# Layer 4 of a conditioned residual stack: expert slots sorted by expert and taken in couples of 256 columns

## The reference

```
x += layer1: expert e = argmax(cond_8[b]):  (silu(x Wup_e + b) * (x Wgate_e + b)) Wdown_e + b    (hidden 256)
x += layer2: x W_base + b + 2 * sum_e cond_8[b,e] * (x A_e) B_e                                  (rank 16)
x += layer3: x (sum_g cond_8[b,g] * weight_g * mask) + bias
x += layer4: sum over the 2 best experts of b: w * (gelu(x Gate_e) * (x Up_e)) Down_e            (hidden 512)
             + the same gated unit with shared weights, for all batches
```

## Time and profile before

| | |
|---|---|
| median of 3 runs | 167.18 us (166.98 to 167.9) |
| the profiled execution, its span | 166.84 us, 165.0 us |
| TensorE busy | 160.8 us (97%) |
| VectorE, ScalarE, GpSimd busy | 84.0 us (51%), 50.0 us (30%), 16.2 us (10%) |
| granted TensorE clock | 1.000 of full |
| DMA | 35.31 MB, mean 214 GB/s |

### The profile page before, as it was taken

How to read it: one execution, slowest core, us unless ns; L and a number is a source line. 1 busy time by engine, 2 the same in 40 slices (tenths; PEclk the granted TensorE clock), 3 DMA queues, 4 the chain that set the end, 5 groups by cost and what they waited for, 6 DMA issues and landing times.

```text
span 165.0 us, 3603 instructions
## 1 busy us (share of the span) xinstructions
PE 160.8 (97%) x1202; PEld 147.9 (90%) x1202; DVE 84.0 (51%) x171; ACT 50.0 (30%) x97; POOL 16.2 (10%) x20
## 2 busy tenths in 40 slices
PE   6999999999999999999999999999999999999994
PEld 2369989999999999999999999999999999999993
DVE  2903665667995362564634364643634563543632
ACT  3656434460542222122222222122222222122120
POOL 2099790000000000000000000000000000000000
PEclk9999999999999999999999999999999999999999
DMA  3999889999801847458684847587494849100001
GB/s 95 405 370 377 318 282 333 312 420 421 368 11 25 344 143 256 183 200 223 223 273 152 308 139 273 182 259 214 174 283 136 319 116 311 44 0 4 0 0 64
DMA packets 8962, 35.31 MB, mean 214 GB/s; under 512 B 1144, under 2 KB 2424, under 8 KB 8824
## 3 DMA queue, kind: packets, MB, share of 16 engines
q1 hardware_dynamic: 8528, 33.99, 59.0%
q10 hardware_dynamic: 424, 1.20, 1.8%
HBM read 34.14 MB, written 1.05 MB: 213 GB/s over the span
## 4 chain that ended last, share of the span: by engine, by line
PE 97%; DVE 1%; issue 0%; POOL 0%; DVEq 0%; POOLq 0%
PE pair L400 35%; PE acc L421 17%; PE pair L393 13%; PE pair L342 9%; PE acc L415 7%; PE acc L351 4%; PE pair L315 3%; PE pair L331 2%; PE pair L372 2%; PE pair L379 2%; PE acc L300 2%; DVE hid L516 0%; PE acc L307 0%; POOL zeros L227 0%; PE acc L326 0%
## 5 line engine op out<-in xcount | busy, mean ns | idle before, releaser
L400 PE MATMUL pair<-x,ring 128*128 (+1 forms) x512 | 62.2, 275 | 0.0
L400 PEld LDWEIGHTS pair<-x,ring 128*128 128x128 f32 x512 | 59.7, 192 | 0.1
L290 ACT ACTIVATE act<-pair 128x512 f32<-128x512 f32 x48 | 28.6, 597 | 85.6 <-PE pair L400 60.3
L563 DVE SCALAR_TENSOR_TENSOR hid<-pair,w_col,act 128x512 f32<-128x512 f32 x32 | 23.9, 751 | 40.2 <-PE pair L400 40.2
L421 PE MATMUL acc<-hid,ring 128*128 128x128 f32 x256 | 33.6, 275 | 0.0
L421 PEld LDWEIGHTS acc<-hid,ring 128*128 128x128 f32 x256 | 32.3, 192 | 1.4
L567 DVE TENSOR_TENSOR hid<-pair,act 128x512 f32<-128x512 f32 x16 | 11.1, 692 | 16.9 <-PE pair L393 16.9
L342 PE MATMUL pair<-x,ring 128*128 x128 | 16.7, 276 | 0.3 <-issue 0.3
L342 PEld LDWEIGHTS pair<-x,ring 128*128 128x128 f32 x128 | 15.5, 192 | 0.5 <-issue 0.5
L516 DVE SCALAR_TENSOR_TENSOR hid<-pair,ring,act 128x128 f32<-128x128 f32 x32 | 9.8, 347 | 9.9 <-PE pair L342 9.7
L279 ACT ACTIVATE act<-pair,ring 128x128 f32<-128x128 f32 x32 | 10.0, 364 | 11.2 <-PE pair L342 11.2
(11 more groups left out here) (62 smaller groups left out, 106.9 us busy)
## 6 DMA issues: line engine op xcount, KB each, us to landing
ring<-experts SPq DMA_DIRECT2D x32, 768.0 KB, 4.4
ring<-experts SPq DMA_DIRECT2D x16, 386.5 KB, 4.6
x<-xT ACTq DMA_DIRECT2D x1, 1024.0 KB, 6.1
shared_sb<-shared SPq DMA_DIRECT2D x1, 768.0 KB, 6.7
out<-x SPq DMA_DIRECT2D x4, 192.0 KB, 4.3
w_sb<-w SPq DMA_DIRECT2D x1, 512.0 KB, 4.0
out<-x SPq DMA_DIRECT2D x4, 64.0 KB, 4.3
small_sb<-small ACTq DMA_DIRECT2D x1, 137.0 KB, 3.9
```

Source lines behind the costliest of these rows:

```text
L290: act.activation(act3[:, u % PAIRS, :], pair[u % PAIRS][0][:, :], ACT.Gelu_apprx_tanh)\
L400: ins = pe.matmul(bank[:, m * P:(m + 1) * P], ring3[:, slot, base + m * P:base + (m + 1) * P], x[:, cols(g * GB + c)], start=True, stop=True)
L563: dve.scalar_tensor_tensor(hid3[:, s, :], pair[s][1][:, :], w_col[:, bass.ds(g * GB + (k[0] * B + c), 1)], act3[:, s, :], ALU.mult, ALU.mu ...
```

## The change

The 32 pairs of batch and expert (slots) are sorted by expert. Each expert's slots are coupled two by two, and what can't be is left single; 12 couples and 8 singles always hold all 32. A couple's two batches are gathered side by side, so that its expert is multiplied with 256 columns in split float32r, in three matmuls for each block of weights. A couple has two units D (two of the four blocks of hidden features each); singles stay R units in float32. Shared units S are as before.

What changes by engine:

- VectorE computes the sort in a chain of small operations after the routing weights, and reads 32 batch numbers into registers ahead of `linear`. In layer 4 it takes the product and the low part of each split unit, and adds each couple's and single's result, times its weight, to `x_sum`, a copy of x.
- TensorE has two matmuls for the ranks, two for the sorted rows, and reads 8 batch numbers.
- SP reads 24 + 8 + 24 numbers, loads 12 + 8 expert packs, gathers 2 x 12 pieces of 128 KB from `x_hl` to `x_duo`, and stores all results at the end.
- ScalarE now rounds all hidden values (`hid_hi`) and the couples' weights (`duo_hi`, three pieces each). GpSimd takes the weights' rest (`duo_lo`) and copies x.
- The loops of layers 1 and 4 are written out.

```diff
+ORDER = _s[:3]
+for _n in range(3):
+    _di, _si, _ri = _d[6 * _n:6 * _n + 6], _s[3 * _n + 3:3 * _n + 6], _r[2 * _n:2 * _n + 2]
+    ORDER += _di[0:2] + _si[0:1] + _ri[0:1] + _di[2:4] + _si[1:2] + _di[4:6] + _ri[1:2] + _si[2:3]
+ORDER += _d[18:20] + _r[6:7] + _d[20:22] + _r[7:8] + _d[22:24] + _s[12:16]
...
+        def values(engine, row, count=B):
+            _, got = nc.values_load_multi_w_load_instructions(
+                row, engines=(engine,), min_val=0, max_val=count - 1, ...)
+            return got
...
 # SP
+            def load_duo(j):
+                if j >= RAWS:
+                    sp.wait_ge(duo_lo_done, 3 * (j - RAWS + 1))
+                sp.dma_start(raw_duo[:, j % RAWS, :], experts3[bass.ds(duo_expert[2 * j], 1), :, :]...)
+            def gather_duo(j):
+                if j >= GATHERS:
+                    sp.wait_ge(up_done, AT["D", j - GATHERS, 1] + 1)
+                for n in range(2):
+                    sp.dma_start(x_duo[:, j % GATHERS, :, n * P:(n + 1) * P],
+                                 x_hl[:, bass.ds(duo_batch[2 * j + n], 1), :, :]...)
+            sp.wait_ge(x_lo_done, G)
+            for j in range(GATHERS):
+                gather_duo(j)
+            for kind, n, part in ORDER:
+                if kind == "R" and n + RAWS < SOLOS:
+                    load_solo(n + RAWS)
+                if kind == "D" and part == 1:
+                    if n + 3 < DUOS:
+                        load_duo(n + 3)
+                    if n + GATHERS < DUOS:
+                        gather_duo(n + GATHERS)
...
 # GpSimd
+            for j in range(DUOS):
+                if j == 1:
+                    for g in range(G):
+                        pool.wait_ge(lin_read, G + g + 1)
+                        pool.tensor_copy(x_sum[:, group(g)], x[:, group(g)]).then_inc(x_copied, 1)
+                for n in range(3):
+                    pool.wait_ge(duo_hi_done, 3 * j + n + 1)
+                    pool.tensor_tensor(duo_lo[...piece(n)], raw_duo[...], duo_hi[...], ALU.subtract)
...
 # ScalarE
+            high_after = {AT["D", j - HALVES, 1] + 3 + n: (j, n) for j in range(HALVES, DUOS) for n in range(3)}
+            high_after.update({n: (1, n) for n in range(3)})
+            for u, unit in enumerate(ORDER):
+                act.wait_ge(gate_done, u + 1)
+                act.activation(act3[:, u % PAIRS, :], pair[u % PAIRS][0][:, :], ACT.Gelu_apprx_tanh)
+                if u in high_after:
+                    duo_high(*high_after[u])
+                if unit[0] != "R":
+                    act.wait_ge(mul_done, u + 1)
+                    act.activation(hid_hi[:, k % SPLITS, :], hid3[:, u % PAIRS, :], ACT.Copy)
...
 # TensorE, gate and up of a D unit
+                elif kind == "D":
+                    pe.wait_ge(x_duo_in[n % GATHERS], 32 * (n // GATHERS + 1))
+                    pe.wait_ge(duo_lo_done, 3 * n + 2)
+                    for bank, base, done in ((gate, GATE3, gate_done), (up, UP3, up_done)):
+                        for i in range(2):
+                            at = slice(base + (2 * part + i) * P, base + (2 * part + i + 1) * P)
+                            for m, (w, h) in enumerate(((duo_hi, 0), (duo_hi, 1), (duo_lo, 0))):
+                                ins = pe.matmul(bank[:, i * N2:(i + 1) * N2], w[:, n % HALVES, at],
+                                                x_duo[:, n % GATHERS, h, :], start=(m == 0), stop=(m == 2))
...
 # VectorE
+            batch = values(mybir.EngineType.DVE, slot_row[0:1, 0:SLOTS])
             dve.wait_ge(x1_done, B)
             for g in range(G):
                 linear(g, g)
...
+            dve.wait_ge(x_copied, G)
+            for u in range(UNITS + 2):
+                if 1 <= u <= UNITS and ORDER[u - 1][0] != "R":
+                    hidden_low(u - 1)
+                if u < UNITS:
+                    dve.wait_ge(act_done, u + 1)
+                    dve.wait_ge(up_done, u + 1)
+                    dve.tensor_tensor(hid3[:, u % PAIRS, :], pair[u % PAIRS][1][:, :], act3[...], ALU.mult)
+                if u >= 2:
+                    result(u - 2)
```

More of the change, by code:

```diff
@@ L166, in cols, with piece @@
             return bass.ds(b * P, P)
-        def x1_value(b):
-            return b + 1
         def group(g):
-            return bass.ds(g * N, N)
+            return slice(g * N, (g + 1) * N)
+        def values(engine, row, count=B):
+            _, got = nc.values_load_multi_w_load_instructions(
+                row, engines=(engine,), min_val=0, max_val=count - 1,
+                skip_runtime_bounds_check_because="batch and expert numbers that the sort has put there itself")
+            return got
+        def piece(n):
+            return slice(n * H3, (n + 1) * H3)
         @block.sync
@@ L180, in _ @@
             sp.dma_start(w2_sb[:, :, :], w2).then_inc(w2_in, 16)
-            def load0(b):
+            sp.wait_ge(at_done, 1)
+            for b in range(B):
+                if b == SLOTS0:
+                    sp.dma_start(shared_sb, shared).then_inc(shared_in, 16)
                 at = sp.value_load(at_row[0:1, b:b + 1], min_val=0, max_val=E - 1)
@@ L200, in store3 @@
[L200 to L205, removed]
-                sp.dma_start(out[:, at], x[:, at]).then_inc(stored, 16)
-            sp.wait_ge(at_done, 1)
-            for j in range(SLOTS0):
-                load0(j)
-            sp.dma_start(shared_sb[:, :], shared).then_inc(shared_in, 16)
@@ new lines, in _ @@
+            for kind, n, part in ORDER:
[6 more added lines that the diff above has]
+                        gather_duo(n + GATHERS)
+            sp.wait_ge(x_summed, SUMMED[ORDER[-1]] - 2)
+            for g in range(G - 1):
+                sp.dma_start(out[:, group(g)], x_sum[:, group(g)]).then_inc(stored, 16)
@@ L225, in _ @@
+            for n in range(2):
+                at = slice((G - 1) * N + n * N2, (G - 1) * N + (n + 1) * N2)
+                sp.wait_ge(x_summed, SUMMED[ORDER[-1]] - 1 + n)
+                sp.dma_start(out[:, at], x_sum[:, at]).then_inc(stored, 16)
+            sp.wait_ge(stored, 16 * (G + 1))
         @block.gpsimd
@@ L353, in down0 @@
                 ins.then_inc(down0_done, 1)
-            pe.wait_ge(pw_done, 1)
             pe.wait_ge(x_in, 16)
-            with pe.Fori(0, STEPS0) as s:
-                upgate0(s, 0)
-                for j in range(SLOTS0):
-                    if j + 1 < SLOTS0:
-                        upgate0(s, j + 1)
-                    down0(s, j)
+            upgate0(0)
+            pe.wait_ge(payload_done, 3)
+            pe.wait_ge(prep_copied, E // 2 + G)
+            for k in range(K):
+                ins = pe.matmul(prep[0][:, 0:3 * SLOTS].rearrange("p (v s) -> p v s", v=3), ones[:, :],
+                                payload[:, :, k, :], start=(k == 0), stop=(k == K - 1))
@@ new lines, in result @@
+            def result(u):
+                unit = ORDER[u]
+                kind, n, part = unit
+                if unit in END_AT:
+                    dve.wait_ge(down_done, u + 1)
+                    dve.wait_ge(x_summed, summed[0])
+                    for i, slot in enumerate(slots_of(unit)):
+                        at = cols(batch[slot])
+                        y = acc[1][:, i * P:(i + 1) * P]
+                        added(dve.scalar_tensor_tensor(x_sum[:, at], y, w_col[:, slot:slot + 1], x_sum[:, at],
+                                                       ALU.mult, ALU.add))
+                elif kind == "S" and part == C3 - 1:
+                    width = N if n < G - 1 else N2
+                    for i in range(N // width):
+                        dve.wait_ge(down_done, u + 1 + i)
+                        if i == 0:
+                            dve.wait_ge(x_summed, summed[0])
+                        at = slice(n * N + i * width, n * N + (i + 1) * width)
+                        added(dve.tensor_tensor(x_sum[:, at], acc[i][:, 0:width], x_sum[:, at], ALU.add))
```

511 lines of the change are left out of this document (307 added, 204 removed).

## The result

| | before | after |
|---|---|---|
| median of 4 runs each | 167.09 us (166.98 to 167.9) | 159.8 us (159.05 to 160.38) |
| ratio, 95% interval | | 0.9551 (0.9493 to 0.9609) |
| profiled execution, span | 166.84, 165.0 | 159.05, 157.3 |
| TensorE busy | 160.8 (97%) | 149.3 (95%) |
| DMA | 35.31 MB | 29.12 MB |

The forecast was 160.5 us and its mechanism was rival A. The page after, in the order of the earlier trace rows: engines, clock in 40 slices, chain.

The account below looks back on a forecast made before the run. TensorE, 97% of the span, was taken as the bound. Terms -13.3 + 0.5 + 1.4 + 1.2 + 1.0 + 1.0 + 1.2 + 0.4 = -6.6 gave a span of 158.4; plus 1.8 and 0.3, 160.5 us, range 155.5 to 168.5.

Parts of the forecast that it names:

- rival A: Whole kernel: TensorE stays the bound, with small stalls; 160.5 us, own range 156.5 to 164.5, chance 0.62.
- TensorE's work in layer 4: Layer 4 matmuls: 24 D units of 2.12 us, layer 105.6 for 118.9, so -13.3 us (-15.9 to -9.9).
- routing: Ahead of layer 1: sort hidden on VectorE, extra rank and payload matmuls not hidden, +0.5 us (-0.4 to +1.3).
- batch numbers on VectorE: Between layer 1 and `linear`: reading 32 numbers as 8 loads, 2.2 us, delays the first split matmul, +1.4 us.
- start of layer 4: TensorE waits before the first S down for product, high part and low part of the hidden values, +1.2 us.
- first gathers: Start of layer 4: two DMAs issued by 47.3 land at 49.5, TensorE asks at 49.4; hidden, no cost.
- steady state: Layer 4's middle: ScalarE and VectorE take turns at 2.16 us a unit, TensorE stays bound; +1.0 us small losses (0 to 5).
- couple 11: Late in layer 4: the last couple's weight piece 1 is made late, so TensorE waits once, +1.0 us.
- adds and stores at the end: After the last down: the add of 256 columns and the landing of 128 KB take longer, +0.4 us.
- Rival B: Batch numbers on VectorE load one at a time, +8.0 us: 167.1 us, no change; chance 0.12.
- Rival C: Layer 4: ScalarE/VectorE turn-taking becomes the bound, low parts standing still beside POOL passes; 185 us at full price, chance 0.11.
- Rival D: Couples' split matmuls of 256 columns stream slower than 512-column ones, 0.235 us each: +50, 211 us; chance 0.07.

## Why the prediction was right

By the sum's steps, in spans (forecast -6.6, measured 157.3 - 165.0 = -7.7):

| step | forecast | measured | from |
|---|---|---|---|
| TensorE's work in layer 4 | -13.3 | -12.9 | D unit 2.14, 24 of them 51.4, layer 106.0 |
| routing | +0.5 | } +0.1 | layer 4 starts 43.41, before 43.34 |
| batch numbers on VectorE | +1.4 | | |
| start of layer 4 | +1.2 | +1.3 | wait ahead of the first S down |
| first gathers | 0, "hidden, and just" | +0.5 | wait ahead of the first couple |
| steady state | +1.0 | +0.0 | 110.5 - 106.0 - 4.2 of waits - 0.3 (below) |
| couple 11 | +1.0 | +1.3 | wait for L344 |
| last down | +1.2 | +1.1 | wait ahead of L545 |
| adds and stores at the end | +0.4 | +1.0 | 153.92 to 157.3, before 162.58 to 165.0 |

The waits stand with their cost from matmul to matmul. The 0.3 is what the layer of before took over its units (119.2 for 118.9). The terms sum to -7.6 by their rounding. The profiled execution was the fastest of the four, so the median comes out at 159.8, 0.7 under the forecast. For the same reason the +0.1 of the first rows is one pair of executions and doesn't settle the routing's +0.5: layer 1 began at 13.24 in this one and up to 1.0 later in the profiles of the experiments. The nearness of the total owes something to luck: 1.3 too much for the batch numbers and 1.0 too much for the steady state stand against 0.6 too little at the end and 0.5 at the gathers.

**TensorE's work.** The midpoint between 0.112 and 0.126 was right: 0.118 forecast, 0.120 measured. The run with 128 columns shows why the lower bound was a poor one: that record isn't paced by its columns, for halving them saved 0.010.

**The batch numbers** are the term that was mis-sized. The time of the load was right by luck (2.2 forecast as eight loads, 2.33 measured as one). The step that failed is "42.4, +1.4": it moved the four adds later with their 3.36 us, but that was TensorE's pace in layer 2, not VectorE's. By the adds' own price, six in 4.37, four take 2.9 us; from 38.29 they end at 41.2, where the fifth add had started at 41.02. The load also began at 35.9, beside the last sum, and not behind it at 36.86. Moving the load confirmed it: nothing came back. Rival B is out, one load fetches all. Here a number costs 73 ns on VectorE (2.33/32) and 59 on SP (1.42/24). The Trainium skill (Runtime: NRT & Kernel Launch, section Instruction fetch mechanics), which I weighed there, has a register load at about 200 ns even for bulk. The trace does not agree for these loads from SBUF; no run shows one from HBM.

**The three waits** were foreseen in place and nearly in size, and three edits, each at one of them, gave 0.41, 0.85 and 0.72 us. That they add shows that they lie on one path, one behind the other.

**The first gathers** weren't hidden. The forecast had both issued by 47.3 and landed at 49.5, with TensorE asking at 49.4. Their price was right (2.2 and 2.3), but SP issued the second only at 47.81; it landed at 50.0, TensorE's weight load followed at 50.04, and 0.4 to 0.5 us were lost. The profile doesn't name the gather, and no run moved it. But in the kernel with the rounding on VectorE the first S down starts at 51.48, after the gathers have landed at 51.3, and there this wait isn't found.

**Steady state.** Nothing was lost there. From the first couple to couple 11, TensorE waits for nothing and its pieces follow each other at their own price. The turn-taking is level with TensorE, as reckoned: at the end, where it is on the chain, from product to product it takes 2.1 us (144.85, 146.96, 149.06, 151.14), for 2.16 forecast. The whole +1.0 for small losses was too much.

Rival C did not come, for the reason given: by the queue's order the low part meets only the end of a POOL pass, with an overlap of 0.16 to 0.35 us where 0.3 was reckoned. It stands still for the overlap less 0.14, so for 0.2 at most and 0.095 in the mean. The danger was real: with the casts further into the passes the kernel was 12.7 us slower than the one after, 7.4 of which went with POOL's passes. The Trainium skill (SBUF — State Buffer, Who interferes with whom) calls what this pair of engines shares an exclusive lock, and counts among its users a VectorE instruction with two SBUF inputs. The traces agree, for the cast and for the low part alike (0.28 and 0.55 us behind the pass, each its own time less 0.14).

**The end** was +1.0, not +0.4. Two adds of 256 columns take 0.78 where one of 128 took 0.29, +0.5, and from the end of the last add to the span's end it is 2.6 us and not 2.1, with two last stores of 128 KB in place of one of 64 KB. I had counted one add, as if the first bank's were hidden; both run in a row, from 153.94 on, while the last downs are still ending.

Rival D is out (0.120, and it decides from 0.133). Expert loads end none of TensorE's waits, and of the gathers, by these times, only the first couple's.

## What to carry to other kernels

Price a matmul by its width before splitting it into more exact parts: here three split products pay only at 256 columns, since 128 columns cost nearly the same. When an engine's start is put off, ask whether its next instructions were paced by it or by their producer; in the second case they catch up, and the delay is free. And once the middle is bound by one engine, look for the waits at the first and last unit and at the last reuse of a buffer: each was worth 0.4 to 0.9 us, and they added. Where one engine's pass makes another stand still, ask how far into the pass the other's instruction begins: here it cost a low part 0.2 us at most and a cast up to 0.85.

## What the runs showed of the hardware

- A VectorE instruction that meets a POOL `tensor_tensor` of 128x512 (1.29 us) stands still until about 0.14 us before the pass's recorded end. This holds for a cast to float32r (1.26 us for 0.43) and for a `tensor_tensor` with both inputs in SBUF (0.84 for 0.69 with an overlap of 0.29, 1.25 with 0.70).
- Two DMAs of 128 KB issued one behind the other on SP start 0.88 us apart (46.93, 47.81) and land 2.3 and 2.2 us after their issue.
- Split matmuls of 128 columns go at 0.110 us, of 256 at 0.120, of 512 at 0.232.
- One register load reads many numbers: 8 in 0.54 us and 24 in 1.42 on SP, 8 in 0.80 on TensorE, 32 in 2.33 on VectorE.
- In the 128-column kernel TensorE's granted clock fell from its upper level to its lower, 1.2 GHz. Windows of 1 us (the stretch, then busy us of PE, PEld, DVE, ACT and POOL with counts, then the clock):

```profile
166.00:167.00 1.00, 0.51 (x5) 0.54 (x5) 0.00 (x0) 0.00 (x0) 0.34 (x1) 1.00 0.00 0
167.00:168.00 1.00, 1.00 (x12) 1.00 (x10) 0.00 (x0) 0.00 (x0) 0.00 (x0) 1.00 0.00 0
168.00:169.00 1.00, 1.00 (x10) 1.00 (x9) 0.00 (x0) 0.95 (x2) 0.00 (x0) 0.80 0.00 0
169.00:170.00 1.00, 1.00 (x6) 1.00 (x6) 0.00 (x0) 0.17 (x1) 0.75 (x1) 0.50 0.00 0
```

TensorE had stood 1.0 us for couple 11 until 166.49, and was busy again when the clock fell, for some 10 us. The same wait of 1.0 in the kernel after was followed by no fall. What made the difference was not tried.
